# A graph kernel: the tail of the first layer inside the edge pass, one product of 150 columns per pair, weight parts added at eviction

## The reference, cut to what matters

```python
h = jnp.maximum(_layernorm(x, axis=-1), 0.0)
# first layer
msg_input = jnp.concatenate([h[src], h[dst], edge_attr], axis=-1)
m = jax.nn.relu(msg_input @ W1.T + b1)
messages = m @ W2.T + b2
agg = jax.ops.segment_sum(messages, dst, num_segments=n)
upd = jax.nn.relu(agg @ Wu.T + bu)
y = h + upd
x = x + layernorm(y) * gamma + beta
h = jnp.maximum(_layernorm(x, axis=-1), 0.0)      # goes into the next layer
# ... three mean layers, three normed mean layers, and two weighted layers:
norm = dinv[src] * w * dinv[dst]
out = jax.ops.segment_sum((h @ W)[src] * norm[:, None], dst, num_segments=n) + b
```

## Time and profile before

| | us |
|---|---|
| median of 3 runs (2385.16 to 2386.99) | 2386.38 |
| the profiled execution | 2400.12 |
| its span, first to last instruction | 2398.6 |
| edge pass, 159.5 to 1393.6 | 1234.1 |
| tail of the first layer, 1404.8 to 1490.2 | 85.4 |
| the layers after it, to the end | 908.4 |

### The profile page before, as it was taken

How to read it: one execution, slowest core, us unless ns; L and a number is a source line. 1 busy time by engine, 2 the same in 40 slices (tenths; PEclk the granted TensorE clock), 3 DMA queues, 4 the chain that set the end, 5 groups by cost and what they waited for, 6 DMA issues and landing times. The chain is left out here.

```text
span 2398.6 us, 31354 instructions
## 1 busy us (share of the span) xinstructions
PE 1557.9 (65%) x10942; PEld 1012.2 (42%) x10942; DVE 957.5 (40%) x2738; ACT 659.2 (27%) x1639; POOL 900.3 (38%) x911
## 2 busy tenths in 40 slices
PE   1405555555555555555455553998978989599997
PEld 1303333434333333334333342675645556445544
DVE  5644454545445454545455446221322124301111
ACT  1303333333333333334333311121323332100000
POOL 5046666666666666666666622000000000000001
PEclk8655666665556666666666655998889989799999
DMA  6423434343443434343343432000100001594571
GB/s 160 119 62 101 119 104 124 109 125 106 112 119 103 124 109 125 107 121 109 106 123 107 121 111 59 1 1 8 41 15 2 5 9 33 191 332 174 200 270 60
DMA packets 203234, 247.43 MB, mean 103 GB/s; under 512 B 36541, under 2 KB 177416, under 8 KB 203061
## 3 DMA queue, kind: packets, MB, share of 16 engines
q1 hardware_dynamic: 174260, 184.35, 24.3%
q0 software_dynamic: 28800, 60.80, 9.7%
HBM read 174.04 MB, written 57.60 MB: 97 GB/s over the span
## 5 line engine op out<-in xcount | busy, mean ns | idle before, releaser
L809 POOL DMA_INDIRECT arena<-dram_PHL,src_of x806 | 823.8, 1022 | 495.0 <-issue 213.2
L1026 PE MATMUL psum<-arena 128*128 128x100 f16 x1568 | 220.9, 247 | 260.0 <-issue 215.0
L1026 PEld LDWEIGHTS psum<-arena 128*128 128x128 f16 x1568 | 174.7, 129 | 392.5 <-issue 370.5
L1010 PE MATMUL psum<-arena 128*128 128x128 f16 x1612 | 209.0, 288 | 180.7 <-issue 146.5
L961 ACT ACTIVATE arena<-psum 128x512 f16<-128x512 f32 x202 | 120.5, 596 | 649.5 <-remote 574.2
L1028 PE MATMUL psum<-arena 128*128 128x50 f16 x1568 | 213.3, 229 | 57.0 <-issue 56.5
L1010 PEld LDWEIGHTS psum<-arena 128*128 128x128 f16 x1612 | 147.6, 130 | 216.4 <-issue 215.8
L2275 POOL DMA_DIRECT2D parts_a<-dram_x x7 | 5.3, 763 | 609.1 <-POOLq L2473 586.0
L880 DVE SCALAR_TENSOR_TENSOR agg_all<-psum,agg_all 128x64 f32<-128x64 f32 x202 | 44.5, 221 | 403.2 <-remote 399.4
L1028 PEld LDWEIGHTS psum<-arena 128*128 128x128 f16 x1568 | 171.5, 114 | 71.1 <-issue 69.8
L869 DVE SCALAR_TENSOR_TENSOR arena<-psum,arena 128x512 f16<-128x512 f32 x202 | 138.4, 685 | 151.7 <-issue 103.8
(11 more groups left out here) (359 smaller groups left out, 2135.3 us busy)
## 6 DMA issues: line engine op xcount, KB each, us to landing
arena<-dram_aw SPq DMA_DIRECT2D x7, 6400.0 KB, 20.4
dram_aw<-arena SPq DMA_DIRECT2D x196, 200.0 KB
arena<-dram_aw SPq DMA_DIRECT2D x3, 4800.0 KB, 17.1
arena<-in_ea_quads SPq DMA_DIRECT2D x51, 256.0 KB
arena<-dram_rel SPq DMA_DIRECT2D x51, 256.0 KB
arena<-arena SPq DMA_DIRECT2D x408, 32.0 KB
arena<-dram_PHL,src_of POOLq DMA_INDIRECT x806
arena<-dram_aw SPq DMA_DIRECT2D x2, 4000.0 KB, 14.8
```

The costliest lines, as they stand in the source:

```text
L809: nc.gpsimd.indirect_dma_start(gathered_p[:, slot, k, :], None, d["PHL"], bass.IndirectOffsetOnAxis(ap=src_of[:, b:b + 1], axis=0)).then_i ...
L1010: nc.tensor.matmul(out[:, k * P:(k + 1) * P], side[:, s, at:at + P], node_side[:, g % NAB, part * D:(part + 1) * D], start=(part == 0 and ...
L1026: nc.tensor.matmul(out, hot_lo[:, u, p, :], hot_key[:, u, p, 0:2].rearrange("p a k -> p (a k)"), start=True, stop=False)
```

## The change

Three things are changed in `edge_pass`, and a phase goes.

The two matmuls of a pair become one of 150 columns into three separate thirds (counts, first and second weight part) of a PSUM bank. The 8 pairs of a window are cut into three units of 3, 3 and 2 pairs, and a ring of 5 banks holds units; `pre` keeps one bank (`NPRE` = 1), the band sums one, and one is for the tail. ACT evicts counts, check and first weight part per unit (nine ops in place of three) and now does so before `relu(s)`; DVE adds the second weight part to the window in SBUF (`whole_weights`, three new ops). The gather ring falls from 6 to 5 groups.

The tail is done inside the pass, per tile of 128 nodes. A tile is due in step `whole_at(t)`, when its sums are complete; the 25 due steps lie 8 or 9 apart. PE's f32 product comes one step later, `update` 2, the root 3, `residual` 4, the next root 5, `normalise` 6, ACT's high part 7 and DVE's low part 8 steps later; SP stores x and loads the nodes of tile t+2 at 6. The tail's weights (8 loads) are loaded at the beginning, and folded in step 2. The pass has 8 more steps at its end. The store of `agg` to DRAM and its load fall away. h of the first layer is kept at the end of `arena`. gamma, beta and the residual move from POOL to DVE.

`first_tail` becomes `crowded_tail`, the same body behind the jump. The cast to `ident_b` moves to the first block of the program.

```diff
+UNIT = 3
+UNITS = -(-PAIRS // UNIT)
+RING = 5
...
 def edge_pass(nc, new, d):
-    NS, NPRE, NPG, NAB = 3, 2, 6, 8
+    NS, NPRE, NPG, NAB = 3, 1, 5, 8
...
+        def bank_of(r, j):
+            return psum[:, 1 + (UNITS * r + j) % RING, 0:len(pairs_of(j)) * 3 * PKEY]
...
         def agg_of(g):
-            return psum[:, 6 + g % 2, 0:BAND]
+            return psum[:, 6, 0:BAND]
+        def whole_at(t):
+            past = EDGE + (t + 1) * P
+            return 1 + max(g for g in range(MG) if base_of(g) + EDGE < past)
+        due = {}
+        for t in range(NT):
+            due[whole_at(t)] = due.get(whole_at(t), []) + [t]
+        LAST = 9
+        def tiles_due(step, behind):
+            return due.get(step - behind, [])
...
             def _(sp):
                 def store_weights(r):
-                    sp.wait_ge(adj_out, r + 1)
+                    sp.wait_ge(weights_out, UNITS * (r + 1))
...
+                def load_nodes(t):
+                    k = t % 2
+                    if t < 2:
+                        sp.wait_ge(folded, 1)
+                    else:
+                        sp.wait_ge(y_varied, t - 1)
+                        sp.wait_ge(v_given, t - 1)
+                        sp.wait_ge(x_stored[k], 16 * (t // 2))
+                    sp.dma_start(h0[:, k], d["h0"][nodes_of(t), :]).then_inc(node_in[k], 16)
+                    sp.dma_start(x[:, k], d["x"][nodes_of(t), :]).then_inc(node_in[k], 16)
+                def store_nodes(t):
+                    sp.wait_ge(x_ready, t + 1)
+                    sp.dma_start(d["x1"][nodes_of(t), :], x[:, t % 2]).then_inc(x_stored[t % 2], 16)
...
                 load_sides(0)
-                for s in range(MG + 1):
+                load_tail_weights()
+                for s in range(MG + LAST):
+                    for t in tiles_due(s, 6):
+                        store_nodes(t)
+                        if t + 2 < NT:
+                            load_nodes(t + 2)
...
-                for q in range(4):
-                    if q == 0:
-                        sp.wait_ge(added, MG)
-                    n = NPAD // 4
-                    sp.dma_start(d["agg"][:, q * n:(q + 1) * n], agg[:, EDGE + q * n:EDGE + (q + 1) * n]).then_inc(
-                        agg_stored, 16)
...
             def _(dve):
                 def pair_hots(r):
-                        dve.wait_ge(multiplied, r - 1)
+                        dve.wait_ge(multiplied, UNITS * (r - 1))
+                def whole_weights(r):
+                    whole = aw_out[:, r % 3, :].rearrange("p (t n) -> p t n", t=NT)
+                    for j in range(UNITS):
+                        dve.wait_ge(halves_out, UNITS * r + j + 1)
+                        nc.vector.scalar_tensor_tensor(out=columns_of_unit(whole, j), in0=third_of(r, j, 2),
+                                                       scalar=1 / UP, in1=columns_of_unit(whole, j), op0=ALU.mult,
+                                                       op1=ALU.add).then_inc(weights_out, 1)
...
+                def update(t):
+                    k = t % 2
+                    dve.wait_ge(fold_read, 2)
+                    step(nc.vector.scalar_tensor_tensor(out=y[:, :], in0=b2u[:, :], scalar=deg_of[:, t:t + 1],
+                                                        in1=bu[:, :], op0=ALU.mult, op1=ALU.add))
+                    dve.wait_ge(u_psum, t + 1)
+                    step(nc.vector.tensor_tensor(y[:, :], psum[:, 7, 0:D], y[:, :], ALU.add))
+                    dve.sem_inc(u_read, 1)
+                    dve.wait_ge(node_in[k], 32 * (t // 2 + 1))
+                    step(nc.vector.scalar_tensor_tensor(out=y[:, :], in0=y[:, :], scalar=0.0, in1=h0[:, k], op0=ALU.max,
+                                                        op1=ALU.add))
+                    step(nc.vector.bn_stats(y_stats[:, :], y[:, :]))
+                    nc.vector.bn_aggr(y_mv[:, :], y_stats[:, :]).then_inc(y_varied, 1)
+                def residual(t):
+                    k = t % 2
+                    dve.wait_ge(y_rooted, t + 1)
+                    step(nc.vector.reciprocal(y_std[:, :], y_std[:, :]))
+                    step(nc.vector.tensor_scalar(y[:, :], y[:, :], y_mv[:, 0:1], y_std[:, 0:1], ALU.subtract, ALU.mult))
+                    step(nc.vector.tensor_tensor(y[:, :], y[:, :], gamma[:, :], ALU.mult))
+                    step(nc.vector.tensor_tensor(y[:, :], y[:, :], beta[:, :], ALU.add))
+                    step(nc.vector.tensor_tensor(x[:, k], x[:, k], y[:, :], ALU.add))
+                    dve.sem_inc(x_ready, 1)
+                    step(nc.vector.bn_stats(x_stats[:, :], x[:, k]))
+                    nc.vector.bn_aggr(x_mv[:, :], x_stats[:, :]).then_inc(x_varied, 1)
+                def normalise(t):
+                    dve.wait_ge(x_rooted, t + 1)
+                    step(nc.vector.reciprocal(x_std[:, :], x_std[:, :]))
+                    nc.vector.tensor_scalar(v[:, :], x[:, t % 2], x_mv[:, 0:1], x_std[:, 0:1], ALU.subtract, ALU.mult
+                                            ).then_inc(v_given, 1)
...
-                for s in range(MG + 1):
+                for s in range(MG + LAST):
                     if s + 1 < MG:
                         hots(s + 1)
                     if s + 1 < J:
                         pair_hots(s + 1)
+                    if 1 <= s <= J:
+                        whole_weights(s - 1)
                     if s < MG:
                         low_parts(s)
-                    if s >= 1:
+                    if 1 <= s <= MG:
                         add(s - 1)
                     if s % QUAD == 2 and s // QUAD + 2 < QUADS:
                         ea_low(s // QUAD + 2)
...
+                    for t in tiles_due(s, 8):
+                        low_of_tile(t)
+                    for t in tiles_due(s, 6):
+                        normalise(t)
+                    for t in tiles_due(s, 4):
+                        residual(t)
+                    for t in tiles_due(s, 2):
+                        update(t)
...
             def _(act):
                 def matrix_out(r):
-                    act.wait_ge(multiplied, r + 1)
                     if r >= 3:
                         act.wait_ge(aw_stored[r % 3], 16 * (r // 3))
...
+                    for j in range(UNITS):
+                        unit = UNITS * r + j
+                        act.wait_ge(multiplied, unit + 1)
+                        nc.scalar.activation(columns_of_unit(flat_adj[:, :, r * W:(r + 1) * W], j), third_of(r, j, 0),
+                                             ACT.Copy, saturate=True)
...
+                        nc.scalar.activation(columns_of_unit(
+                            aw_out[:, r % 3, :].rearrange("p (t n) -> p t n", t=NT), j), third_of(r, j, 1), ACT.Copy,
+                            scale=1 / UP).then_inc(halves_out, 1)
...
-                for s in range(MG + 1):
+                for s in range(MG + LAST):
+                    if 1 <= s <= J:
+                        matrix_out(s - 1)
                     if s < MG:
                         relu(s)
-                    if 1 <= s <= J:
-                        matrix_out(s - 1)
...
             def _(pe):
                 def multiply(r):
                     u = r % 2
                     pe.wait_ge(hot_keys, r + 1)
-                    if r >= 2:
-                        pe.wait_ge(adj_out, r - 1)
-                    for p in range(PAIRS):
-                        out = pair_of(r, p)
-                        nc.tensor.matmul(out, hot_lo[:, u, p, :], hot_key[:, u, p, 0:2].rearrange("p a k -> p (a k)"),
-                                         start=True, stop=False)
-                        done = nc.tensor.matmul(out[:, PKEY:2 * PKEY], hot_lo[:, u, p, :], hot_key[:, u, p, 2],
-                                                start=False, stop=True)
-                    done.then_inc(multiplied, 1)
+                    for j in range(UNITS):
+                        unit = UNITS * r + j
+                        if unit >= RING:
+                            pe.wait_ge(weights_out, unit - RING + 1)
+                        for i, p in enumerate(pairs_of(j)):
+                            thirds = bank_of(r, j).rearrange("p (q x) -> p q x", q=3)
+                            done = nc.tensor.matmul(thirds[:, :, i * PKEY:(i + 1) * PKEY], hot_lo[:, u, p, :],
+                                                    hot_key[:, u, p], start=True, stop=True)
+                        done.then_inc(multiplied, 1)
...
+                def update_product(t):
+                    pe.wait_ge(added, whole_at(t))
+                    at = slice(EDGE + t * P, EDGE + (t + 1) * P)
+                    nc.tensor.matmul(psum[:, 7, 0:D], agg[:, at], w2u[:, :], start=True, stop=True).then_inc(u_psum, 1)
...
-def first_tail(nc, new, d):
+def crowded_tail(nc, new, d):
```

More of the change, by code:

```diff
@@ L72 @@
 H1, M2 = 2 * D, 48
+H_FIRST = NT * NCOL - NT * 2 * D
 LN_EPS = 1e-5
@@ L669, in edge_pass, with own @@
         sb = carve
```

(21 more changed lines are left out.)

444 lines of the change are left out of this document (264 added, 180 removed).

## The result

The changed kernel takes 2434.43 us (median of 4 runs, 2425.29 to 2445.03) against 2385.91 us before: ratio 1.0205, with an interval of 1.016 to 1.0249. It is slower; the forecast was 2331 us and faster. (2385.91 is the median of four runs; the table ahead of the prediction has three of them.) The profiled execution took 2425.29 us with a span of 2423.7.

The account below looks back on a forecast made before the run. It took a loop through SP's queue (18.5 us) plus PE instruction starvation (6 us) to bound the 24.44 us quad. 2400.1 - 75 + 2 + 18 = 2345 profiled, 13.7 less for the median: 2331 us; own range 2255 to 2392.

Parts of the forecast that it names:

- part 1: Tail phase after the edge pass removed: 98.1 us between last add and wide layer becomes 23, saving 75 us.
- parts 3 to 5: Edge pass: DVE additions, ACT's units and order make the quad 21.3 us; tail ops add 2.0, SP's waits 0.7.
- SP's waits for nodes: Edge pass, SP queue: tail's node loads wait behind normalise and delay loads or stores, mean 1.5 us a tile, 0.7 a quad.
- part 2: Edge pass, PE: one product per pair, 65 instructions a step against 78, ends most instruction starvation, leaving 0.8 us a quad.
- the 6 us: Edge pass: share of the 24.44 us quad beyond the loop's 18.5, read as PE running out of instructions.
- 0.8 us left: Edge pass: PE starvation taken to remain per quad, since the stores' traffic starves PE too.
- the bounds: Edge pass: 0 to 3 us a quad of PE starvation could be left.
- Rival 1: Edge pass: gaps come from DMA traffic, about 3 of 6 us stay, quad 27.0, 2442 us, slower; chance 0.22.
- eight instructions per 0.72 us: Edge pass, PE: starved supply pace, letting some 130 instructions through the 11.8 us window after the side loads.
- loop sum of 18.5: Edge pass before the change: loop over SP's queue, ACT, PE and DVE costs 18.5 us a quad without other loss.
- rival 2: Edge pass: PE's stream was the limit, DVE has room; quad falls to 21.5 us, 2165 us; chance 0.08.
- Rival 3: Edge pass: SP's waits for nodes cost near 3.8 us in every tile, +57, 2388 us, no change; chance 0.12.

Follow-up runs that it names:

- set B: Follow-up set, without stalls: unchanged copies of both kernels, the tail alone moved into the pass, and extra TensorE waits; kernel before 2210.8 us.
- c_after: Unchanged copy of the changed kernel, rerun without stalls beside the kernel before: 2251.77 us, ratio 1.0204, quad 23.37 us.
- c_before: Unchanged copy of the kernel before, rerun without stalls: one run, 2213.18 us, quad 21.06 us.
- the first set: The original measurement, with stalls: kernel before 2385.91 us, changed kernel 2434.43 us, ratio 1.0205.
- set D: Follow-up set, with stalls: copies of the kernel before, the changed kernel, the product without the tail, and the moved store; kernel before 2387.03 us.
- d_product: Kernel before with the 150-column product, units, DVE additions, single bank, five gather groups and new ACT order, tail in its own phase: 2561.44 us, ratio 1.0735.
- the sets without stalls: The four follow-up sets in which the kernel before takes 2210 to 2213 us, against 2386 to 2387 us in the two with stalls.
- set E: Follow-up set, without stalls: kernel before without the 50-column product (0.9997) and with extra met TensorE waits (1.0026); kernel before 2209.71 us.
- b_extra_waits: Kernel before with 32 already-met TensorE waits written per step, 16 instructions run: 2215.26 us, ratio 1.0026.
- a_relu_first: Changed kernel with ACT's old order, relu ahead of the units: 2421.43 us, ratio 1.0945, quad 26.79 us.
- sets C and D: Two follow-up sets: C loosened the changed kernel's loop, kernel before 2212.65 us; D repeated four kernels, kernel before 2387.03 us.
- a_store_first: Changed kernel with SP's store of a step ahead of that step's loads: 2138.17 us, ratio 0.9672, quad 20.79 us.

## Why the prediction was wrong

**The removed phase (part 1): right.** 23 us were forecast between the last `add` and the wide layer, 24.7 came; 75 saved against 73.4. In set B the stretch from the last load of edge data to the end is 78 us shorter in c_after than in c_before (1040.9 to 962.9).

**The loop and its terms (parts 3 to 5): right in form, 0.6 us high.** L780 to ACT's release: forecast 5.2, measured 5.1 in the first set and 5.2 in c_after (medians). L780 to L791: 9.4 forecast, 9.4 and 9.5 measured (medians). The additions: 0.85 in sequence against 0.70 busy. SP's waits for nodes are there (86.2 us at L822 over 500 to 1000 us of c_after). Without the gaps the forecast's quad is 21.3 + 2.0 + 0.7 = 24.0 us; set B, which has none, measures 23.37. The small ACT ops overlap: in the first timeline the third unit begins 1.44 us after the first, 0.72 us a unit, where the forecast had 0.68.

**The gaps (part 2): wrong, and this is the step that failed.** "So most of the 6 us goes, by this reckoning all", with 0.8 us left. By the forecast's own measure (the pass over 50.5) the changed kernel's quad is 1333.7 / 50.5 = 26.41 us, against 24.8 forecast; 1.6 x 50.5 = 81 us more, and 2345 + 81 = 2426 is the profiled execution (2425.29). Of the 26.41, 23.4 are there without gaps, so 3.0 us of them were left, the upper end of the bounds; 3.3 by SP's loads (26.64), and 3.9 in set D (27.28). The term was too small by 2.2 us a quad, 111 us in all, of which the loop's 0.6 gave 30 back. (The median lies 9 us above the profiled execution here, where before it lay 14 below; that is the rest.) Rival 1, with 3 of the 6 us left and 2442 us, names this outcome; it had a chance of 0.22. Its cause, that the DMA traffic by itself makes the gaps, is not borne out: c_before moves 133 GB/s over 500 to 1000 us with no stall, the kernel before in the first set 113 with them. Nor does any run show what the 0.8 us stood on, that the traffic of the stores starves TensorE.

Why the reckoning failed: its pace of "eight instructions per 0.72 us" isn't in the earlier trace rows, which have one matmul (with its weight load) in that time, and it took the gaps for a supply that TensorE's stream of instructions draws on, so that fewer instructions would end them. d_product speaks against that. It has the new kernel's 65 instructions a step and no tail, and its quad is 27.54 us in set D where 21.07 suffice without gaps: at least 6.5 us of gaps. The kernel before, with 78 a step, has 24.43 there; by the forecast's own loop sum of 18.5 that is 5.9 us. Fewer instructions left as much. In the sets without stalls, 62 and 94 instructions a step make 0.999 and 1.003. And the signals of TensorE that come 4 us behind records already made are not what a lack of instructions ahead of it would look like; that is argued and not tested. The transfers of instructions were no slower either: queue q8 moved 106 packets of them in 1.14 us each (mean) both in the first trace and in c_before. The one clean test, those two kernels in a set with stalls, is missing: set E was of the other kind. The forecast also rests on the earlier trace rows alone, on one engine; the waits of ACT and DVE on "remote" stood in the same trace (574.2 us before L961). What makes the stalls, and so why about 3 us of them stayed, is open.

The Trainium skill, page "Runtime: NRT & Kernel Launch", section "Instruction fetch mechanics", says that fetching runs by itself and is mostly hidden. For the sets without stalls b_extra_waits agrees (1.0026 with 20% more instructions). The forecast had named it for rival 1 and set it aside on two rows.

**What the forecast didn't look for.** It worked out the loop with three buffers, saw that the store hangs behind `load_edges`, and then treated the loop as given. A quad bounded by POOL at 21 us and a loop at 24 leave 3 us for whoever loosens the loop: with the store moved, the change is worth 0.967 in place of 1.020 without stalls, and 0.983 in place of 1.025 with them. It also missed the loop that a_relu_first exposes. Of the kernels with the whole change, only those with the loosened loop came near rival 2's quad of 21.5 (20.79 and 20.97). Rival 3's condition, SP's waits for nodes, is fulfilled (86.2 us), but they cost little. In both traces of the changed kernel 14 of the 47 quads have L791 more than 11 us after L780; they last 27.65 us on average against 26.21 for the other 33 in the first set, and 24.38 against 22.94 in c_after. Spread over all quads that is 0.4 us, an estimate from these means; the forecast had 0.7 and the rival some 1.1 more.

## What to carry to other kernels

Where an engine waits for a store, find the queue that issues the store and what stands ahead of it there: if that is a load that waits for the same engines, the two form a loop, and work added to any member lengthens it. Two moved lines or one more buffer can be worth more than the change under test, and parts of a change that each cost next to nothing (1.0022 and 0.9663 without stalls) can cost 2% together once their loop passes the bound that hid it. Before the end of a stall is credited to a change, look at every engine that shows it and at the signal that ends each wait; a gap whose cause isn't known stays in the sum in full. And count the instructions that an edit meant to add: 32 waits written were 16 instructions run.

## What the runs showed of the hardware

The same kernel before takes 2383 to 2389 us in two sets of runs (2400 in the first profiled execution) and 2202 to 2221 us in four, each set agreeing within 1%. The difference lies in the edge pass (24.43 and 24.66 us a quad against 21.06) and comes with waits that end at late signals of TensorE: the relu starts 3.9 and 4.4 us (median) behind the record of its product, against 0.04 in c_before. The chip's number doesn't decide it: sets C and D carry the same number. The mean granted clock over the span of the kernel before was 0.738 to 0.74 in the profiled executions with stalls and 0.772 in c_before; POOL's gathers took nearly the same time in both (1.02 and 1.01 us apiece on average over 500 to 1000 us, with 0.30 between). What causes the stalls is open; I had no kernel that brings them about. They lengthen a quad by 3.4 us in the kernel before, 4.1 in a_store_first, 3.9 in the changed kernel and 6.5 in d_product, each against the same kernel in a set without them; part of that difference may stay hidden where POOL's pace leaves room.

ACT's ops on 150 columns out of PSUM are recorded with 0.29 to 0.58 us, but a unit of four of them (L1110, L1115 with its read of the accumulator, L1118) starts every 0.7 us.
